# Reordered engine programs and bf16 filler matmuls in the first stage of a graph-attention and mixture-of-experts kernel

## The reference

```python
# x: 128 graphs x 64 nodes x 128 features (8192 tokens), adj: 64 x 64
x = x + gnn(layernorm(x), adj, W, a)          # graph attention inside each 64-node graph
x = x + moe(layernorm(x), Wg, bg, W1, b1, W2, b2)

def gnn(h, adj, W, a):
    Wh = h @ W
    e = Wh @ a[:D] + swapaxes(Wh @ a[D:], 1, 2)
    e = where(adj > 0, where(e > 0, e, 0.2 * e), -inf)
    return elu(softmax(e) @ Wh)

def moe(x, ...):                               # 8 experts, hidden 512, the best 2 by gate score
    score = x @ Wg.T + bg
    combine = softmax over the two best scores, placed at their experts
    return sum_e combine[e] * (relu(x @ W1[e].T + b1[e]) @ W2[e].T + b2[e])
```

## Time and profile before

| what | value |
|---|---|
| median of 3 runs | 505.11 us (505.02 to 507.4) |
| the profiled execution | 506.94 us, of which the span from first to last instruction is 505.1 us |
| mean granted TensorE clock | 0.871 |
| TensorE busy | 400.2 us (79%) |
| VectorE busy | 372.2 us (74%) |
| ScalarE busy | 322.9 us (64%) |
| GpSimd busy | 289.7 us (57%) |
| chain that ended last | TensorE 55%, issue 11%, ScalarE 11%, VectorE 9%, GpSimd 5%, DMA 5% |

### The profile page before, as it was taken

How to read it: one execution, slowest core, us unless ns; L and a number is a source line. 1 busy time by engine, 2 the same in 40 slices (tenths; PEclk the granted TensorE clock), 3 DMA queues, 4 the chain that set the end, 5 groups by cost and what they waited for, 6 DMA issues and landing times.

```text
span 505.1 us, 9093 instructions
## 1 busy us (share of the span) xinstructions
PE 400.2 (79%) x2030; PEld 313.8 (62%) x2044; DVE 372.2 (74%) x1416; ACT 322.9 (64%) x760; POOL 289.7 (57%) x283
## 2 busy tenths in 40 slices
PE   3868887779877786509999999999999999999000
PEld 2645655667665564407887878778787878888000
DVE  6479999887789877544777777686777777777914
ACT  2568788776777767305777777676776767777000
POOL 0002777666656765765366656666665666566564
PEclk9889999775588769557999999999999999999755
DMA  5585333322222322343223232323223232227987
GB/s 135 163 326 162 94 98 96 90 86 84 78 78 84 90 86 79 94 129 104 64 84 103 81 100 76 96 80 105 79 84 100 84 106 84 74 84 258 346 247 241
DMA packets 55068, 59.73 MB, mean 118 GB/s; under 512 B 7553, under 2 KB 40705, under 8 KB 54785
## 3 DMA queue, kind: packets, MB, share of 16 engines
q1 hardware_dynamic: 36880, 35.41, 23.6%
q0 software_dynamic: 8704, 17.97, 10.8%
q10 hardware_dynamic: 9456, 6.06, 4.0%
HBM read 26.75 MB, written 24.28 MB: 101 GB/s over the span
## 4 chain that ended last, share of the span: by engine, by line
PE 55%; issue 11%; ACT 11%; DVE 9%; POOL 5%; DMA 5%; SPq 1%; ACTq 1%; POOLq 0%; DVEq 0%
PE bank L1189 6%; POOL moe_rows L499 5%; PE bank L1172 5%; PE bank L1176 5%; PE bank L1173 5%; PE bank L1186 5%; PE bank L1187 5%; PE bank L1092 4%; PE bank L1115 3%; ACT xn L617 3%; PE bank L1076 3%; PE bank L1133 3%; PE bank L1153 3%; PE bank L1161 2%; ACT prob L572 2%
## 5 line engine op out<-in xcount | busy, mean ns | idle before, releaser
L486 POOL DMA_INDIRECT expert_slots<-rows,slot_i x128 | 126.3, 987 | 105.3 <-DVE slot_i L771 69.0
L499 POOL DMA_INDIRECT moe_rows<-hrelu,ysi x40 | 43.1, 1076 | 38.4 <-DVE ysi L989 20.2
L999 DVE CAST hh<-z 128x512 fp32r<-128x512 f32 x36 | 18.1, 502 | 58.2 <-ACT z L656 58.2
L1186 PE MATMUL bank<-hh,w_hi 128*128 128x512 f32 x144 | 60.4, 420 | 0.0
L665 ACT ACTIVATE yb<-bank,b_sb 128x512 f32<-128x512 f32 x36 | 24.8, 689 | 54.1 <-PE bank L1189 54.1
L1172 PE MATMUL bank<-xh,w_hi 128*128 128x512 f32 x144 | 58.0, 402 | 0.8 <-ACT xh L642 0.8
L1189 PE MATMUL bank<-hl,w_hi 128*128 128x512 f32 x144 | 58.1, 404 | 0.1
L1176 PE MATMUL bank<-xl,w_hi 128*128 128x512 f32 x144 | 57.5, 399 | 0.0
L1173 PE MATMUL bank<-xh,w_lo 128*128 128x512 f32 x144 | 57.5, 399 | 0.0
L1187 PE MATMUL bank<-hh,w_lo 128*128 128x512 f32 x144 | 56.9, 395 | 0.0
L499 POOL DMA_INDIRECT moe_rows<-u,ysi x32 | 39.1, 1222 | 23.6 <-issue 12.9
(11 more groups left out here) (153 smaller groups left out, 1063.1 us busy)
## 6 DMA issues: line engine op xcount, KB each, us to landing
xs<-expert_slots SPq DMA_DIRECT2D x36, 260.0 KB, 2.7
rows<-xn SPq DMA_DIRECT2D x32, 256.0 KB
x_all<-x SPq DMA_DIRECT2D x16, 256.0 KB, 2.9
w_raw<-w_t SPq DMA_DIRECT2D x2, 2048.0 KB, 12.1
w_raw<-moe_rows SPq DMA_DIRECT2D x16, 256.0 KB, 5.7
out<-x_all ACTq DMA_DIRECT2D x16, 256.0 KB, 3.6
w_hi<-moe_rows SPq DMA_DIRECT2D x9, 256.0 KB, 4.5
expert_slots<-rows,slot_i POOLq DMA_INDIRECT x128
```

The lines of the kernel that those rows point to most:

```text
L486: nc.gpsimd.indirect_dma_start(out=slots, out_offset=bass.IndirectOffsetOnAxis(ap=slot_i[q][:, k * SUB + j:k * SUB + j + 1], axis=0), in_= ...
L499: nc.gpsimd.indirect_dma_start(out=moe_rows, out_offset=bass.IndirectOffsetOnAxis(ap=ysi[b][:, t:t + 1], axis=0), in_=ys[b][:, t, :], in_o ...
L1186: nc.tensor.matmul(ps_y[:, :], w2_hi[:, e, c, :], hh[:, c, :], start=c == 0, stop=False)
```

## The change

Only the first stage and the moment before the second are touched.

- TensorE: three matmuls of 128x512 in bf16 (identity times mask) are written into ps_tp ahead of the softmax transposes, whenever there is a g1; eight into ps_t3 ahead of the transposes of xn2; 45 into ps_z once table_ok has come. Their results are never read: the banks are overwritten by what follows. wh stands ahead of the xn2 transposes instead of behind them.
- ScalarE: high_halves stands between the softmax exponentials and the copy prob_t (before: at the step's end), in steps 9 to 16 (before: 7 to 14). L591 and L593 stand ahead of the copy xn1_t (before: behind gap_e). The copy wh stands ahead of the copy xn2_t.
- VectorE: within a step the order was statistics of a later group (bn3), ranks, u, x_all, slot_i, score, maximum, statistics bn2, token numbers, aggregates and variances, first normalization. It becomes ranks, slot_i, bn3, u, score, maximum, x_all, bn2, first normalization, token numbers, aggregates and variances. What follows (logits and so on) is as before. low_halves runs in steps 10 to 17.
- by_steps unrolls ten steps instead of eight; the loop covers steps 10 to 13.

```diff
+FILL_STEP, FILL_NORM, FILL_TABLE = 3, 8, 45
+HIGH, LOW = 9, 10
...
-            for t in range(E):
+            for t in range(LOW):
                 at(t)
-            with eng.Fori(E // 2, GROUPS // 2 - 1) as m:
+            with eng.Fori(LOW // 2, GROUPS // 2 - 1) as m:
...
         ScalarE, step(): behind the exponentials
+                if not isinstance(t, int):
+                    high_halves(2 * m + (q - HIGH))
+                elif 0 <= t - HIGH < E:
+                    high_halves(t - HIGH)
                 if g1 is not None:
                     act.wait_ge(prob_ps, g1 + 1)
...
                     nc.scalar.copy(prob_t[:, :, :], tiles(ps_tp)).then_inc(prob_t_ok, 1)
+                if gx is not None:
+                    act.wait_ge(var2_ok, gx + 1)
+                    n = norms(gx)
+                    nc.scalar.activation(log2_v[:, 0:n, :], var2[:, 0:n, :], ACT.Ln).then_inc(log2_ok, 1)
+                    act.wait_ge(log2_ok, gx + 1)
+                    nc.scalar.activation(root2[:, 0:n, :], log2_v[:, 0:n, :], ACT.Exp, scale=-0.5).then_inc(root2_ok, 1)
                 if g0 is not None:
                     act.wait_ge(xn1_ps, g0 + 1)
...
         (the same five lines and the four of high_halves are taken out further down,
          and the copies of wh and xn2_t change places)
...
         VectorE, step(): the end of the new order up to the first normalization
+                if gx is not None and norms(gx) > 1:
+                    dve.wait_ge(x_in[q], 16 * (m + 2))
+                    for j in range(SUB):
+                        nc.vector.bn_stats(bn3[:, j, :], x_all[:, bass.ds(gx + AHEAD, 1), j, :].rearrange("p g d -> p (g d)"))
+                if gx is not None:
+                    dve.wait_ge(hrelu_ok, gx + 1)
+                    dve.wait_ge(hexp_ok, gx + 1)
+                    nc.vector.scalar_tensor_tensor(u[:, :, :], hrelu[:, :, :], 1.0, hexp[:, :, :], ALU.add, ALU.min
+                                                   ).then_inc(u_ok, 1)
...
-                    low_halves(2 * m + (q - E))
-                elif E <= t < 2 * E:
-                    low_halves(t - E)
+                    low_halves(2 * m + (q - LOW))
+                elif 0 <= t - LOW < E:
+                    low_halves(t - LOW)
...
         TensorE
+            def fill(tile, n):
+                for _ in range(n):
+                    nc.tensor.matmul(tiles(tile), ident_b[:, :], mask_b[:, :, :], start=True, stop=True)
...
                     if later(g1):
                         pe.wait_ge(prob_t_ok, g1)
+                    fill(ps_tp, FILL_STEP)
                     for j in range(SUB):
                         pe.wait_ge(exp_ok, SUB * g1 + (j + 1))
...
         (wh, unchanged, now stands here, ahead of the xn2 transposes)
                 if gx is not None:
+                    if later(gx):
+                        pe.wait_ge(xn2_t_ok, gx)
+                    fill(ps_t3, FILL_NORM)
+                    for j in range(SUB):
+                        pe.wait_ge(xn2_ok, SUB * gx + (j + 1))
+                        last = nc.tensor.transpose(tiles(ps_t3)[:, j, :], xn2[q][:, j, :], ident)
+                    last.then_inc(xn2_ps, 1)
...
             by_steps(pe, step)
+            pe.wait_ge(table_ok, 1)
+            pe.wait_ge(z_ok, GROUPS)
+            fill(ps_z, FILL_TABLE)
             bounds = block_bounds(pe)
```

More of the change, by code:

```diff
@@ L587, in step @@
                     nc.scalar.activation(gap_e[:, :], gap[:, :], ACT.Exp).then_inc(gape_ok, 1)
[L588 to L593, removed]
                 if g1 is not None:
@@ L618, in step @@
                                              scale=rstds[:, bass.ds(gx, 1), 0, j]).then_inc(xn2_ok, 1)
+                if g0 is not None:
+                    act.wait_ge(wh_ps, g0 + 1)
+                    nc.scalar.copy(wh[:, :, :], tiles(ps_wh)).then_inc(wh_ok, 1)
                 if gx is not None:
@@ L623, in step @@
                     nc.scalar.copy(xn2_t[:, :], ps_t3[:, :]).then_inc(xn2_t_ok, 1)
-                if g0 is not None:
-                    act.wait_ge(wh_ps, g0 + 1)
-                    nc.scalar.copy(wh[:, :, :], tiles(ps_wh)).then_inc(wh_ok, 1)
                 if isinstance(t, int) and t + 1 < len(BATCHES):
                     first_root(t + 1)
[L629 to L632, removed]
             by_steps(act, step)
@@ L729, in step @@
                     first_stats(0)
[L730 to L733, removed]
                 if gr is not None:
@@ L751, in step @@
                                             ).then_inc(base_ok, 1)
[L752 to L764, removed]
                 if gr is not None:
@@ L784, in step @@
                     nc.vector.tensor_reduce(neg_max[:, :], score[:, :, :], AX, ALU.max, negate=True).then_inc(neg_ok, 1)
+                if gx is not None:
+                    dve.wait_ge(u_ok, gx + 1)
+                    nc.vector.scalar_tensor_tensor(x_all[:, bass.ds(gx, 1), :, :].rearrange("p g s d -> p (g s) d"),
+                                                   u[:, :, :], -1.0,
+                                                   x_all[:, bass.ds(gx, 1), :, :].rearrange("p g s d -> p (g s) d"),
+                                                   ALU.add, ALU.add).then_inc(x2_ok, 1)
+                if gx is not None:
+                    dve.wait_ge(x2_ok, gx + 1)
+                    dve.sem_inc(met, 1)
                 for j in range(SUB):
@@ L790, in step @@
                             last.then_inc(stats2_ok, 1)
+                if g0 is not None:
+                    if isinstance(t, int) and t < len(BATCHES):
+                        first_rstd(t)
+                    if isinstance(g0, int) and g0 < AHEAD:
+                        dve.wait_ge(rstd1_ok, 1 + (g0 >= BATCHES[1].start))
+                        rstd_of, mean_of = rstd1[:, g0:g0 + 1, :], mv1[:, g0:g0 + 1, :, 0]
+                    else:
+                        dve.wait_ge(rstd2_ok, g0 - AHEAD + 1)
+                        dve.wait_ge(mean1_ok, g0 - AHEAD + 1)
+                        rstd_of, mean_of = rstds[:, bass.ds(g0 - AHEAD, 1), 1, :], mean1[:, bass.ds(g0, 1), :]
+                    if later(g0):
+                        dve.wait_ge(xn1_ps, g0)
+                    for j in range(SUB):
+                        nc.vector.tensor_scalar(xn1[:, j, :], x_all[:, bass.ds(g0, 1), j, :].rearrange("p g d -> p (g d)"),
+                                                mean_of[:, :, j], rstd_of[:, :, j],
+                                                ALU.subtract, ALU.mult
+                                                ).then_inc(xn1_ok, 1)
                 if gx is not None:
@@ L814, in step @@
                                               ).then_inc(mean1_ok, 1)
[L815 to L832, removed]
                 if gl is not None:
@@ L1119, in step @@
                     last.then_inc(z_ps, 1)
[L1120 to L1126, removed]
                 if g0 is not None:
```

1 line of the change is left out of this document (removed).

## The result

The changed kernel takes 490.52 us (median of 6 runs, 489.74 to 492.64) against 504.99 us before; the ratio is 0.971 (95% interval 0.969 to 0.974). The forecast was 494.8 us (487.5 to 502.0). Ratios compare the faster executions of each kernel, those within 1.5% of its fastest. The profiled execution took 490.51 us, with a span of 488.7 us, 16.4 less than before.

What follows compares the result with a forecast made beforehand. First stage bound by VectorE early, later by a chain with TensorE at half clock; second by TensorE. Reordering and later halves -14.1, falls +2.6, last steps -0.8, 45 fillers +2.3, start -0.3: -10.3, giving 494.8 us (487.5 to 502).

Steps and rivals of the forecast that it cites:

- rival B: Whole kernel: the clock never falls in the steps and the 45 fillers are free; 488.7 us, chance 0.20.
- the nine steps: First stage, exponentials of step 7 to those of step 16: 115.69 us before, forecast to change by -14.1 + 2.6.
- Two falls at 1.3 us, +2.6: Nine steps of the first stage: two clock falls remain despite fillers, each costing 1.3 us; bounds 0 to +11.7.
- the step at 11.70 us: First stage before the change: heavy step (both halves) from 145.13 to 156.83, taken as nearly full clock to price falls.
- sparse stretch: TensorE, end of the eight fillers to av in heavy steps: only three fillers as wide work, so some falls remain.
- Steps 10 to 15 at 11.6 us each: First stage, steps with both halves, bound by VectorE: 10.38 + 1.21 us each, part of the nine steps' 101.6.
- The start, -0.3: Steps 1 and 2, where two falls stood before: a quarter of one fall saved, bounds -2.6 to 0.
- The reordering at 0, behind nearly unbroken VectorE: Nine steps: the new order itself costs or gains nothing; bounds +3.5 us and 0.9 us below nothing.
- The last steps, -0.8: Step 16 to the table's end: high halves +1.04, gates at full clock -1.7, transposes -0.1; at half clock up to +4.4.
- The 45 fillers, +2.3: Between the stages: fillers end 5.3 us past the rows, a full-clock start saves 2.8; bounds +0.3 to +3.3.
- A: First stage: the sparse stretch brings the clock down in every step, nine falls cost 11.7 us; 503.9 us, chance 0.16.
- C: First stage: fillers at half clock make TensorE the bound, steps of about 15 us; 514 us, chance 0.09.

Runs made afterwards that it cites:

- e1: The changed kernel without its 45 fillers between the stages (three and eight per step stay): 486.31 us, ratio 0.963 to the kernel before.
- e5: The changed kernel without the 45 fillers, halves in steps 7 to 14 and 8 to 15: 575.8 us on a chip where the kernel before took 593.7.
- e3: The kernel before, in its old order, with three fillers ahead of the softmax transposes and eight ahead of the xn2 transposes: 496.25 us, ratio 0.984.
- e6: The changed kernel without the 45 fillers and with VectorE's step order of before: 490.52 us, ratio 0.973; 592.8 and 580.1 us on slower chips.

## Why the prediction was right, and which terms were off

*The mechanism held, the number partly by luck.* The range holds 490.5, but it lies nearer to rival B's 488.7 than to the forecast's 494.8. Against the forecast's terms the nine steps came out 6.9 us better, the start 2.8 and the rest 0.6; the last steps came out 1.7 and the 45 fillers 2.45 us worse. The errors offset in part.

What held is that the clock was a large cause and that fillers keep it: 10.4 us of the nine steps had been put down to falls, and the fillers alone gave 10.0.

*Two falls at 1.3 us, +2.6.* There was one fall, and it cost next to nothing. It made its own step longer, 13.13 us (130.08 to 143.21) against 11.66 in e1, but the next one took 10.18 instead of 11.42 (143.21 to 153.39, against e1's 141.92 to 153.34). Over the nine steps it is 97.3 against 97.1 us. VectorE hardly noticed. Its maximum in step 13, in the changed kernel and in e1:

```profile
141.01 0.69 DVE L776 TENSOR_REDUCE neg_max<-score 128x4 f32<-128x512 f32 x1
```
```profile
140.97 0.69 DVE L776 TENSOR_REDUCE neg_max<-score 128x4 f32<-128x512 f32 x1
```

So in these steps, which VectorE bounds, one short fall (135.6 to 139.0) fits into the other engines' slack. The 1.3 us was an average over eight falls with 58 us of half clock in 116 us, and is no price of a single one. Its base, the step at 11.70 us, also had 3.4 us of half clock in it.

Why the clock fell just there isn't shown. The forecast named this sparse stretch (though it expected the fall ahead of av and not behind it), and TensorE waits there for VectorE's choice of experts:

```profile
124.00 0.19 PE L1108 MATMUL bank<-chosen_b,before_b 128*128 128x32 bf16 x1 [1.44 <-DVE chosen_b L873]
...
135.87 0.20 PE L1108 MATMUL bank<-chosen_b,before_b 128*128 128x32 bf16 x1 [1.43 <-DVE chosen_b L873]
```

But the step before has the same wait and no fall, and so has e1 (1.44, 1.37 and 1.14 us in three steps).

*Steps 10 to 15 at 11.6 us each* is the term that was mis-sized most. In e1, with no fall, the nine steps take 97.1 us where 101.6 were forecast. Steps 11 to 13 fit: 11.89, 11.66, 11.42. The interval that begins with step 10 is 10.55, since there was slack to use up: in step 10 of e1 the exponentials start 1.3 us behind the end of the maximum (106.52 and 107.82), in step 11, behind the first low halves, at its end (118.34 and 118.37). Those of steps 14 and 15 are 10.30 and 10.11. I had overlooked what VectorE no longer does there. From step 14 on the group four ahead doesn't exist, and bn3 is gone. In the changed kernel's step 12 it stands ahead of u; in e1's step 14 it doesn't:

```profile
126.91 0.22 DVE L756 TENSOR_REDUCE slot_i<-slot_p 128x8 int32<-128x64 f32 x1
127.17 0.87 DVE L761 BATCH_NORM_STATS2 bn<-x_all 128x6 f32 x4
127.96 0.67 DVE L766 SCALAR_TENSOR_TENSOR u<-hrelu,hexp 128x512 f32<-128x512 f32 x1
```
```profile
150.23 0.22 DVE L756 TENSOR_REDUCE slot_i<-slot_p 128x8 int32<-128x64 f32 x1
150.37 0.68 DVE L766 SCALAR_TENSOR_TENSOR u<-hrelu,hexp 128x512 f32<-128x512 f32 x1
```

That is 0.8 us, and with its four aggregates, by my estimate, about 1.2 us, as much as low halves add. Steps 14 and 15 are 2.8 us below the forecast together; 0.7 of the rest is step 9, at 10.50 instead of 11.2. That moving the halves there is worth this much is argued from these rows: e5, which was to test it, decided nothing.

*The start, -0.3,* was -3.1. Both early falls of the kernel before are gone, and I had given that a quarter of one. e3, in which they are gone too but the order is the old one, gained 1.7 us at the start; the other 1.4 go with the new order. The lower bound, -2.6, had the falls alone.

*The reordering at 0, behind nearly unbroken VectorE,* was too little. e6 puts VectorE's order at some 4 us over the whole kernel (3.8 on the same chip, its own fall included), where I had bounds of 3.5 us for a loss and 0.9 for a gain. My test was whether VectorE stays busy; what e6 shows is that in the old order ScalarE waits for the maximum with the exponentials in some heavy steps.

*The last steps, -0.8,* were +0.9: there is a fall at 176.6, and e1 without it took 25.0 us, still 0.4 over the 24.5 before. The last gate takes 1.06 us as hoped (191.70), but in e1 too the clock falls, at 184.8. The eight fillers then run at half clock, and TensorE turns to the xn2 transposes 1.3 us after the last xn2 tile (188.7), the case for which the forecast had its upper bound:

```profile
186.60 3.57 PE L1075 MATMUL bank<-mask_b,ident_b 128*128 128x512 bf16 x8
...
189.97 1.06 PE L1144 MATMUL bank<-cst,xn 128*128 128x128 f32 x4
```

*The 45 fillers, +2.3,* were +4.75. Their length was nearly right: they ended at 211.5, 12.1 us behind the table's end at 199.40, against 12.6; the clock rose 4.5 us behind the first of them, where I had 5. (5.3 - 2.8 is 2.5, and not the 2.3 that I took.) Two things were not in the sum. The transposes started 1.4 us after the last filler, 6.1 us later behind the table than before. And the clock fell again at 214.1, so only 1.4 of the 2.8 us of a warm start came: 5.8 us from the first transposes to the next, against 7.15 before.

Of the rivals, A (a fall in every step) and C (fillers feed on half clock) did not occur in any profiled execution with fillers on the 505 us chips. B's number, 488.7, is nearest to e1's 486.3, which has what B assumed: no fall in the nine steps, and no cost between the stages. What B had wrong is that the 45 are free.

## What to carry to other kernels

Where a granted clock below 1 stands over a stage with short waits on TensorE, fill the waits with work into banks that are about to be overwritten; here wide bf16 matmuls and dense float32 transposes did equally well over the nine steps. It must end before the real operand arrives. Price half clock over a whole stage with and without fillers, and not by one step: a step that a fall lengthens can be made up by the next. Behind the last filler count what else is queued there, register loads too. And when work is moved to other iterations of a software pipeline, list what each engine does in each of them: the last ones lack a part, and that may be room.

## What was not expected of the hardware

Dense float32 transposes of 128x128 (14 in 1.69 us) held the clock at 2.4 GHz over nine steps as 512-column bf16 matmuls did. A wait of 1.43 us on TensorE stood at a fall, and waits of 1.44, 1.44 and 1.37 us at the same place of other steps stood at none. One program without fillers took 491.2 to 505.3 us on one chip, and its mean granted clock ran with it, 0.870 to 0.842. With the loads of the eight block bounds ahead of it, TensorE's first filler came 5.7 us behind the table, while behind 45 fillers the same loads left a gap of 1.4 us. Two of the chips ran the kernel before in 583 and 594 us instead of 505; the variants traced there had waits of up to 7 us, from step 4 on, that no engine of the core explains.
